# Epsilon and the normalising step of ten norms move to VectorE, only the power stays on GpSimd, and the order of all engines is laid out anew

## What is computed

```python
x = x + tanh(g_xattn[0]) * _L0_xattn_ref(ctx, _layernorm(x), ...)   # cross attention, 8 heads
x = x + tanh(g_ffn[0])   * _L0_ffn_ref(_layernorm(x), ...)          # two layers of local attention, norm, gelu MLP
x = x + tanh(g_xattn[1]) * _L1_xattn_ref(_layernorm(x), ctx, ...)   # rmsnorm, linear, patches picked from ctx
x = x + tanh(g_ffn[1])   * _L1_ffn_ref(_layernorm(x), ...)          # top-2 of 8 experts of rank 16
x = x + tanh(g_xattn[2]) * _L2_xattn_ref(ctx, _layernorm(x), ...)   # attention over ctx, 8 heads
x = x + tanh(g_ffn[2])   * _L2_ffn_ref(_layernorm(x), ...)          # ternary MLP, activations rounded to 8 bits
x = x + tanh(g_xattn[3]) * _L3_xattn_ref(_layernorm(x), ctx, ...)   # attention, 16 heads, 128 keys
x = x + tanh(g_ffn[3])   * _L3_ffn_ref(_layernorm(x), ...)          # ternary, conv over 3 rows, silu, ternary
# _layernorm(x) = (x - mean) / sqrt(var + 1e-5), over the 128 features
# the rounding: xq = round(x * 127 / max|x|) * max|x| / 127, per row
```

## Time and profile before

| | before |
|---|---|
| median of 3 runs | 1790.29 us (1786.92 to 1790.97) |
| the profiled execution, its own time | 1793.24 us |
| its span, first to last instruction | 1791.5 us |
| busy: PE, DVE, ACT, POOL | 1561.3, 1269.6, 1099.3, 927.9 us |
| ACT_TABLE_LOAD | 70, 1283 ns each |

### The profile page before, as it was taken

How to read it: one execution, slowest core, us unless ns; L and a number is a source line. 1 busy time by engine, 2 the same in 40 slices (tenths; PEclk the granted TensorE clock), 3 DMA queues, 4 the chain that set the end, 5 groups by cost and what they waited for, 6 DMA issues and landing times.

```text
span 1791.5 us, 44987 instructions
## 1 busy us (share of the span) xinstructions
PE 1561.3 (87%) x17452; PEld 1046.9 (58%) x17452; DVE 1269.6 (71%) x3220; ACT 1099.3 (61%) x2248; POOL 927.9 (52%) x1784
## 2 busy tenths in 40 slices
...
GB/s 155 55 11 20 31 32 33 33 24 20 26 33 34 33 34 33 32 33 33 21 25 25 34 33 33 33 34 32 33 33 4 23 24 24 24 23 24 22 14 3
DMA packets 78035, 55.08 MB, mean 31 GB/s; under 512 B 44665, under 2 KB 70649, under 8 KB 77566
## 3 DMA queue, kind: packets, MB, share of 16 engines
...
## 4 chain that ended last, share of the span: by engine, by line
issue 44%; POOL 31%; POOLq 20%; SPq 1%; PE 1%; ACT 1%; DMA 1%; DVE 1%
POOLq L608 12%; POOL wide_a L465 10%; POOL rden L465 10%; POOLq L606 4%; POOL back L613 4%; POOL rstd L465 2%; POOLq L630 1%; POOL far L579 1%; POOLq L578 1%; POOLq L588 1%; POOL far L581 1%; SPq L411 1%; POOL patches L465 1%; POOL pick L465 1%; SPq L406 1%
## 5 line engine op out<-in xcount | busy, mean ns | idle before, releaser
L465 POOL TENSOR_TENSOR rstd<-mv,ln_eps 128x1 f32<-128x1 f32 x320 | 89.3, 279 | 639.4 <-DVE mv L1033 349.0
L465 POOL TENSOR_TENSOR rstd<-rstd,minus_half 128x1 f32<-128x1 f32 x320 | 203.3, 635 | 46.6 <-issue 1.7
L465 POOL TENSOR_TENSOR rden<-rden,minus_half 128x16 f32<-128x16 f32 x64 | 188.3, 2943 | 9.4
L956 DVE TENSOR_REDUCE mx<-ps_all 128x8 f32<-128x512 f32 (+1 forms) x192 | 166.0, 864 | 27.9 <-PE ps_all L1261 10.5
L465 POOL TENSOR_TENSOR wide_a<-wide_a,wide_b 128x256 f32<-128x256 f32 x256 | 177.8, 726 | 0.0
L1239 PE MATMUL ps_all<-ident,wide_b 128*128 128x128 f32 x1024 | 155.4, 285 | 17.7 <-ACT wide_b L726 7.1
L706 ACT COPY wide_a<-ps_all 128x512 f32<-128x512 f32 (+1 forms) x192 | 133.4, 725 | 55.8 <-PE ps_all L1239 34.0
L1239 PEld LDWEIGHTS ps_all<-ident,wide_b 128*128 128x128 f32 x1024 | 111.5, 143 | 70.3 <-issue 49.8
L1361 PE MATMUL ps_all<-ht,w 128*128 128x128 f32 x768 | 151.8, 327 | 0.1
L669 ACT ACT_TABLE_LOAD x70 | 89.8, 1283 | 99.6 <-PE ps_all L1361 83.8
L1361 PEld LDWEIGHTS ps_all<-ht,w 128*128 128x128 f32 x768 | 130.8, 214 | 11.2 <-issue 0.6
...
## 6 DMA issues: line engine op xcount, KB each, us to landing
...
```

The costliest lines, as they stand in the source:

```text
L465: return gp.tensor_tensor(o, a, b, op)
L956: v.tensor_reduce(most, of, AX.X, ALU.max).then_inc(*done(f"{n}_max"))
```

## The change

`inv_std` on POOL is the power alone. Adding epsilon is a DVE stage, `_eps` (ten of them; the norm of the patches stays as it was); `normalise` is a DVE instruction, (x - mean) x rstd, or two of 64 columns in l0f0 and l0f1. l2f and l3f take `centre`, x - mean, into the rounding, and rstd goes into the step (`_step`, a stage of its own) by which the rounded numbers are multiplied. `small2` of l1f is made on DVE. The tiles `back` and `ln_eps2` go. All tables of order and the table of banks have new numbers.

```diff
@@ POOL
-                def inv_std(n, eps=ln_eps):
+                def inv_std(n):
                     yield f"{n}_rstd"
-                    tile(f"{n}_var")
-                    tt(rstd[:, s:s + 1], mv[:, s, 1:2], eps[:], ALU.add)
-                    gp.drain()
-                    tt(rstd[:, s:s + 1], rstd[:, s:s + 1], minus_half[:, 0:1], ALU.pow)
-                    gp.drain()
-                    if n == "l1f":
-                        n_op = gp.tensor_scalar(small2[:, s:s + 1], rstd[:, s:s + 1], gate[:, 5:6], 0.5, ALU.mult,
-                                                ALU.mult)
-                    else:
-                        n_op = gp.tensor_scalar(back[:, s:s + 1], mv[:, s, 0:1], rstd[:, s:s + 1], -1.0, ALU.mult,
-                                                ALU.mult)
-                    n_op.then_inc(*done(f"{n}_rstd"))
+                    tile(f"{n}_eps")
+                    tt(rstd[:, s:s + 1], rstd[:, s:s + 1], minus_half[:, 0:1], ALU.pow).then_inc(*done(f"{n}_rstd"))
@@ ACT
-                def normalise(n, of=None):
-                    yield f"{n}_y"
-                    tile(f"{n}_rstd")
-                    a.activation(y[:, s, :], x[:, s, :] if of is None else of, ACT.Identity, scale=rstd[:, s:s + 1],
-                                 bias=back[:, s:s + 1]).then_inc(*done(f"{n}_y"))
@@ DVE
+                def above_zero(n, eps=LN_EPS):
+                    yield f"{n}_eps"
+                    tile(f"{n}_var")
+                    ts(rstd[:, s:s + 1], mv[:, s, 1:2], eps, None, ALU.add).then_inc(*done(f"{n}_eps"))
+                def normalise(n, of=None):
+                    yield f"{n}_y"
+                    tile(f"{n}_rstd")
+                    ts(y[:, s, :], x[:, s, :] if of is None else of, mv[:, s, 0:1], rstd[:, s:s + 1], ALU.subtract,
+                       ALU.mult).then_inc(*done(f"{n}_y"))
+                def centre(n):
+                    yield f"{n}_y"
+                    tile(f"{n}_var")
+                    ts(y[:, s, :], x[:, s, :], mv[:, s, 0:1], None, ALU.subtract).then_inc(*done(f"{n}_y"))
@@ absmax
-                    v.reciprocal(small2[:, s:s + 1], small[:, s:s + 1])
-                    ts(small[:, s:s + 1], small[:, s:s + 1], tern_step[:, step:step + 1], None, ALU.mult
-                       ).then_inc(*done(f"{n}_inv"))
+                    v.reciprocal(small2[:, s:s + 1], small[:, s:s + 1]).then_inc(*done(f"{n}_inv"))
+                    yield f"{n}_step"
+                    tile(f"{n}_inv")
+                    if n in ("l2f", "l3f"):
+                        tile(f"{n}_rstd")
+                    ts(small[:, s:s + 1], small[:, s:s + 1], tern_step[:, step:step + 1],
+                       rstd[:, s:s + 1] if n in ("l2f", "l3f") else 1.0, ALU.mult, ALU.mult).then_inc(*done(f"{n}_step"))
@@ BANK_TABLE
 l0a_sc 6 2 l0a_sub
-l0f1_ot 4 1 l0f1_ots
+l0f1_ot 7 1 l0f1_ots
-l3a0_sc 5 2 l3a0_sub
-l3a1_sc 0 2 l3a1_sub
+l3a0_sc 3 2 l3a0_sub
+l3a1_sc 4 2 l3a1_sub
```

More of the change, by code:

```diff
@@ L43 @@
 PE_TIMES = """
[L44 to L48, removed]
@@ L49 @@
[L49 to L51 removed]
+    l0a_kv 1875, l0a_yt 1967, l0a_q 1974, l0a_sc 2026, l0a_pt 2103, l0a_pv 2205, l0a_ot 2254, l0a_out 2258,
+    l0f0_yt 2281, l0f0_qk 2304, l0f0_v 2401, l0f0_qkt 2435, l0f0_sc 2448, l0f0_pt 2534, l0f0_pv 2556, l0f0_ot 2618,
@@ new lines @@
+    l0f0_wo 2630, l0f0_sh 2718, l0f0_lt 2777, l0f0_hid 2840, l0f0_out 2880, l0f1_yt 2915, l0f1_qk 2935, l0f1_v 2935,
+    l0f1_qkt 3046, l0f1_sc 3062, l0f1_pt 3104, l0f1_pv 3124, l0f1_ot 3185, l0f1_wo 3203, l0f1_sh 3260, l0f1_lt 3321,
+    l0f1_hid 3351, l0f1_out 3386, l1a_yt 3467, l1a_out 3472, l1f_yt 3517, l1f_lg 3524, l1f_ot 3568, l1f_out 3584,
+    l2a_yt 3647, l2a_sc 3663, l2a_pt 3691, l2a_pv 3726, l2f_qt 3784, l2f_hid 3842, l2g_qt 3928, l2g_out 3968,
+    l3a_yt 4029, l3a_qkv 4053, l3a0_sc 4080, l3a1_sc 4086, l3a0_pt 4116, l3a0_pv 4138, l3a1_pt 4180, l3a1_pv 4185,
@@ L113 @@
-l0f1_yt 6 1 l0f1_hs
-l0f1_qk 6 2 l0f1_turned
-l0f1_v 0 2 l0f1_vs
-l0f1_qkt 2 2 l0f1_qts
-l0f1_sc 3 2 l0f1_sub
-l0f1_pt 4 1 l0f1_pts
-l0f1_pv 0 2 l0f1_o
-l0f1_ot 4 1 l0f1_ots
-l0f1_wo 1 1 l0f1_y1
-l0f1_sh 6 1 l0f1_y
-l0f1_lt 5 1 l0f1_lts
-l0f1_hid 0 2 l0f1_gated
-l0f1_out 7 1 l0f1_x
-l1a_yt 5 1 l1a_ht
-l1a_out 5 1 l1a_x
-l1f_yt 3 1 l1f_ht
-l1f_lg 0 1 l1f_o
-l1f_ot 7 1 l1f_ots
-l1f_out 0 1 l1f_x
-l2a_yt 5 1 l2a_ht
-l2a_sc 0 2 l2a_sub
-l2a_pt 4 1 l2a_pts
-l2a_pv 1 2 l2a_o
-l2f_qt 3 1 l2f_qts
-l2f_hid 5 1 l2f_pre
@@ new lines @@
+l0f0_sc 5 2 l0f0_sub
+l0f0_pt 0 1 l0f0_pts
+l0f0_pv 4 2 l0f0_o
+l0f0_ot 1 1 l0f0_ots
+l0f0_wo 5 1 l0f0_y1
+l0f0_sh 2 1 l0f0_y
+l0f0_lt 0 1 l0f0_lts
+l0f0_hid 5 2 l0f0_gated
+l0f0_out 4 1 l0f0_x
+l0f1_yt 7 1 l0f1_hs
+l0f1_qk 5 2 l0f1_turned
+l0f1_v 1 2 l0f1_vs
+l0f1_qkt 0 2 l0f1_qts
+l0f1_sc 2 2 l0f1_sub
+l0f1_pt 3 1 l0f1_pts
+l0f1_pv 0 2 l0f1_o
+l0f1_ot 7 1 l0f1_ots
+l0f1_wo 3 1 l0f1_y1
+l0f1_sh 3 1 l0f1_y
+l0f1_lt 3 1 l0f1_lts
+l0f1_hid 1 2 l0f1_gated
+l0f1_out 4 1 l0f1_x
+l1a_yt 3 1 l1a_ht
+l1a_out 6 1 l1a_x
```

172 lines of the change are left out of this document (94 added, 78 removed).

## The result

| | before | after |
|---|---|---|
| median | 1790.63 us (1786.92 to 1792.18, 4 runs) | 1820.09 us (1814.06 to 1821.44, 4 runs) |
| span of the profiled execution | 1791.5 us | 1817.3 us |
| ratio | | 1.0152, 95% interval 1.0126 to 1.0178 |

The change makes the kernel 1.5% slower. I had forecast slower, and 1860: the direction and the range hold, the loss is 29 us and not 70.

A forecast was written before the change was run, and what follows sets the result against it. PE's work sets the pace, 49.4 us a tile. Waiting of 5.15 us in place of 2.6, plus 0.5 for the clock, gives 26 x 3.0 = 78 us, less 8 at the ends: 1860 us, range 1805 to 1935.

The forecast's parts named there:

- The norms: Norm from end of bn_aggr to end of y: 1.92 us falls to 1.14; 9 us saved along one tile's chain.
- The ends: Filling and draining, where few tiles are in flight: shorter norms save 8 us, between 4 and 12.
- first place: l3a1_sc shares a bank with l3a0_sc, so PE waits for DVE's l3a0_sub: 1.9 us a tile.
- second place: l0f1_ot takes the bank l0a_sc held, so PE waits for DVE's l0a_sub: 1.2 us a tile.
- third place: 64 more ACT table loads around l1f_tanh make PE wait at l1f_ot, l3a1_pt and l0f1_sc: 1.15 us a tile.
- small waits: PE waits elsewhere in the new order, at copies with little PE work behind them: 0.9 us a tile.
- The clock: PE's granted clock falls as PE waits more: 0.5 us a tile, between 0 and 2.5.
- beside PE's work: DVE's added 4.6 us a tile alone costs PE no time, though it fills gaps where DVE caught up.
- PE hides it all: Rival: DVE and ACT run far ahead, steady part keeps 49.4 us a tile, ends give 8 us: 1782; chance 0.08.
- no change: Rival: a few short PE waits of 0.3 us a tile eat up the gain: 1790; chance 0.03.
- A mild loss: Rival: one of the two bank-sharing waits is real and the other isn't: 1795 to 1815; chance 0.05.
- The lower clock and the drain: Rivals: granted clock falls further, 1930 to 2000, or table switches drain ACT besides loading, 1932; chance 0.08 together.

The follow-up runs named there:

- e9: The changed kernel with all order and bank numbers chosen anew so that the longest circuit through the engines is short; 1714.29 us, 0.9576.
- e10: The kernel before, its arithmetic kept, with order and bank numbers chosen anew so that no circuit through the engines is long; 1739.33 us, 0.9715.
- e1_scores_bank: The changed kernel with l3a1_sc on banks 5 and 6 and l1f_lg on bank 7, so l3a1_sc needn't wait for l3a0_sub; 1815.48 us, 1.0141.
- e3_no_switch: The changed kernel with an exponential in place of l1f_tanh, so 64 fewer table loads (leaves out the tanh); 1804.88 us, 1.0077.
- e2: The changed kernel with l0f1_ot on bank 2 in place of 7, so it needn't wait for l0a_sub; 1816.98 us, 1.015.
- e4: The changed kernel with l3a1_sc, l1f_lg and l0f1_ot on other banks and an exponential in place of l1f_tanh; 1805.24 us, 1.007.
- e5_old_order: The changed arithmetic in the order and banks of the kernel before, new stages put into DVE's list; 1.0141, median 1817.44 us.

## Why the prediction was right in sign and too large in size

**The norms.** Right. From the end of bn_aggr to the end of y a norm now takes 1.2 us, where I had 1.14 and the earlier trace rows show 1.92:

```profile
69.73 0.18 DVE L917 BATCH_NORM_AGGREGATE mv<-stats 128x2 f32<-128x6 f32 x1
...
70.77 0.35 DVE L929 TENSOR_SCALAR y<-x,mv,rstd 128x128 f32<-128x128 f32 x1 [0.66 <-POOL rstd L465]
```

The ends gave 5 us (I had 4 to 12, taken at 8), in e9 against e10 some 18.

**The places.** Right as to where PE waits, with no size below what was measured:

| | forecast, us a tile | measured |
|---|---|---|
| first place (L1503, and both rows of L1324) | 1.9 | (20.8 + 5.6 + 3.0) / 19.8 = 1.5 |
| second place (L1258 <- DVE) | 1.2 | 12.5 / 19.8 = 0.6 |
| third place (L1251, and L1258 <- ACT wide_a) | 1.15 | (9.1 + 2.3) / 19.8 = 0.6 |
| small waits | 0.9 | the rest of 3.6: 0.9 |
| sum | 5.15 | 3.6 |

This is the mis-sized term: (5.15 - 3.6) x 26 = 40 us, nearly the whole miss. For the first two places the path through DVE was right, and PE's own work beside it was reckoned too short. PE's rows at the first place, in which l0f1_qk starts at 1076.21 and l3a1_sc at 1085.65:

```profile
1076.21 1.98 PE L1316 MATMUL ps_all<-w_qkv,ht_shift 128*128 128x512 f32 x4
1078.35 1.94 PE L1324 MATMUL ps_all<-w_qkv,ht_shift 128*64 128x512 f32 x8 [0.16 <-DVE wide_b L1002]
...
1082.03 1.94 PE L1324 MATMUL ps_all<-w_qkv,ht_shift 128*64 128x512 f32 x8 [0.47 <-ACT wide_c L725]
...
1085.65 0.66 PE L1503 MATMUL ps_all<-wide_a,qt 32*64 32x512 f32 x4 [1.04 <-DVE wide_b L948]
```

From 1076.21 to 1085.65 are 9.44 us. I had 8.95 for the path through DVE, the trace has 9.3 to the end of l3a0_sub. I had 7.0 for PE's work; less the three waits it is 7.8. A sum of start-to-start times out of another order (1.77 for l0f1_qk, say, where 2.0 pass here) is too short by what stands between the stages here; why they follow each other less closely in this order, no run shows. This turn is also one of those in which l0f1_sq started late, behind the transfer of v_pad, so that its second wait is 0.47 us; in e1_scores_bank it is 0.18. At the second place DVE took 6.7 us, as forecast to the tenth, and PE's work was 5.9 in place of 5.5. A wait that is a difference of two long sums takes up every error of both.

**The tables.** 0.6 us of waiting for 1.15, and e3_no_switch prices both loads at 15 us, 0.6 us a tile, of which 0.23 is in a turn at full clock. That is the lower half of my range. In the chain above the last load takes from 991.48 to 992.76 us and the exponential starts at 992.77. The Trainium skill, page ScalarE: Activation LUTs, section What ACT_TABLE_LOAD costs, adds a drain of 1.38 us to the 1.28 of the load: for 64 switches 64 x 2.66 = 170 us of ACT (an estimate by that page). The trace agrees on the load (1283 ns) and not on the drain: in e3_no_switch ACT is busy 80.9 us less than in the changed kernel (984.5 and 1065.4), 1.26 for each load, and the exponential waits 0.01 us behind it.

**The clock.** Wrong in sign: I took 0.5 us a tile more for it, 13 us in all. A mean turn is 0.5 us above one at full clock in the changed kernel (50.6 and 50.13) and 0.7 in the kernel before (49.4 and 48.73), so the clock gave back some 0.2 us a tile, though PE waits more. From 1600 to 1700 us it is 0.96 where the earlier trace rows have 0.80.

**The step that failed beneath these sizes** is the one that took each place as a loss of its own: "any place where its next stage's input comes later than now adds straight to 49.4 us". e1, e2 and e4 took two of the three waits away; at full clock the first gave nothing and the second 0.16 us a tile. And the step that let DVE's 4.6 us lie "beside PE's work" failed with e5_old_order: nothing of the new order was in it, and a turn at full clock took 0.53 us longer. These errors have opposite signs. With DVE's work at 26 x 0.53 = 14 us the forecast would have been some 1874, further off; that it wasn't is luck.

**The rivals.** PE hides it all, and no change, are out. "A mild loss, between 1795 and 1815" was next to the measured time, but by its condition (one of two places real, the other not) it isn't what happened. The lower clock and the drain are out.
